# Edge convolution on one core: x picked in two exact float32r parts by two matmuls a tile, node keys in SBUF, narrow sums, 20 picked steps, a ring of six

## What is computed

```python
xn  = (x - mean) * rsqrt(var + 1e-5) * gamma + beta
feat = concatenate([xn[dst], xn[src] - xn[dst]], axis=-1)       # (200000, 128)
msg = relu(feat @ W1 + b1) @ W2 + b2                            # (200000, 64)
agg = segment_max(msg, dst, num_segments=6250); agg = where(isfinite(agg), agg, 0)
out = layernorm(x + relu(agg))                                  # over the 64 channels
```

## Time and profile before

| | |
|---|---|
| median of 3 runs | 1803.86 us (1803.62 to 1804.23) |
| the profiled execution | 1801.84 us, its span 1800.1 us |
| PE | 1721.3 us busy (96%) |
| POOL | 1317.6 us (73%) |
| DVE | 1197.9 us (67%) |
| ACT | 939.6 us (52%) |
| mean granted clock of TensorE | 0.977 of full speed |

### The profile page before, as it was taken

One profiled execution on the slowest core, in us unless ns is written; L12 is line 12 of the kernel. 1 busy time (PEld: TensorE's weight loads), 2 busy tenths in 40 slices (PEclk: granted clock), 3 DMA queues, 4 the chain that ended last, 5 costly groups with the idle time before them and its releaser, 6 DMA issues.

```text
span 1800.1 us, 26957 instructions
## 1 busy us (share of the span) xinstructions
PE 1721.3 (96%) x9871; PEld 851.8 (47%) x9871; DVE 1197.9 (67%) x1951; ACT 939.6 (52%) x1111; POOL 1317.6 (73%) x1388
## 2 busy tenths in 40 slices
PE   4489999999999999999999999999999999999995
PEld 3244444444444444444444444444445445444442
DVE  5556676666766766667667667676676676666753
ACT  4545555545455545555555555555555555555553
POOL 7777777777777777777777777777777777777722
PEclk8589999999999999999999999999999999999998
DMA  7633343334334333343343333343333433343320
GB/s 180 176 94 93 67 98 88 75 82 96 79 82 97 72 96 79 86 96 67 85 94 96 83 82 93 73 95 70 97 89 65 104 83 85 79 99 81 70 55 5
DMA packets 131566, 156.85 MB, mean 87 GB/s; under 512 B 74988, under 2 KB 76969, under 8 KB 131400
## 3 DMA queue, kind: packets, MB, share of 16 engines
q1 hardware_dynamic: 85674, 109.73, 19.6%
q0 software_dynamic: 44464, 45.18, 17.0%
q10 hardware_dynamic: 1294, 0.20, 0.1%
HBM read 147.24 MB, written 9.39 MB: 87 GB/s over the span
## 4 chain that ended last, share of the span: by engine, by line
PE 94%; DVE 2%; SPq 1%; DMA 1%; ACT 1%; ACTq 1%; issue 0%; POOLq 0%; POOL 0%; DVEq 0%
PE ps_g L1074 29%; PE ps_g L1081 15%; PE ps_acc L1149 11%; PE ps_mr L1118 11%; PE ps_h L1140 10%; PE ps_mr L1124 5%; PE ps_h L1133 5%; PE ps_x L1110 4%; PE ps_h L1138 2%; DMA src_t<-in_src 1%; DMA a_dram<-oh 1%; DVE runmax L939 0%; PE ps_x L1037 0%; SPq L336 0%; SPq L351 0%
## 5 line engine op out<-in xcount | busy, mean ns | idle before, releaser
L473 POOL DMA_INDIRECT xs<-in_x,src_ix x1372 | 1304.8, 951 | 420.4 <-issue 417.3
L865 DVE TENSOR_SCALAR oh<-ps_k 128x1024 bf16<-128x1024 bf16 x1176 | 731.9, 679 | 0.8
L1074 PE MATMUL ps_g<-oh,xtab 128*128 128x512 bf16 x2352 | 541.1, 380 | 0.0
L635 ACT ACTIVATE rows<-ps_mr 128x512 f32<-128x512 f32 x196 | 116.8, 596 | 554.5 <-PE ps_mr L1124 545.1
L939 DVE TENSOR_TENSOR_SCAN runmax<-rb,runmax,ps_mr 128x512 f32<-128x512 bf16 x196 | 250.6, 1278 | 181.2 <-PE ps_mr L1118 180.3
L1074 PEld LDWEIGHTS ps_g<-oh,xtab 128*128 128x128 bf16 x2352 | 217.0, 98 | 301.9 <-issue 68.9
L640 ACT ACTIVATE hid<-ps_h,bias 128x1024 f32<-128x1024 f32 x196 | 218.2, 1113 | 175.0 <-PE ps_h L1140 139.1
L1081 PE MATMUL ps_g<-oh,xtab 128*64 128x512 bf16 x2352 | 289.7, 383 | 0.0
L922 DVE TENSOR_TENSOR best<-ps_acc,last_key 128x336 f32<-128x336 f32 x196 | 99.5, 508 | 282.0 <-PE ps_mr L1124 264.2
L1149 PEld LDWEIGHTS ps_acc<-rows,best 128*106 128x106 f32 x1568 | 183.0, 172 | 160.1 <-issue 155.8
L596 ACT ACTIVATE best<-best,ones 126x1024 bf16<-126x1024 bf16 x196 | 225.1, 1149 | 6.4
(11 more groups left out here) (162 smaller groups left out, 584.6 us busy)
## 6 DMA issues: line engine op xcount, KB each, us to landing
kb<-keys_dram SPq DMA_DIRECT2D x98, 504.0 KB
rb<-reset_dram SPq DMA_DIRECT2D x98, 256.0 KB
xs<-in_x,src_ix POOLq DMA_INDIRECT x1372
src_t<-in_src SPq DMA_DIRECT2D x48, 256.0 KB, 6.7
aw<-a_dram SPq DMA_DIRECT2D x196, 31.5 KB
a_dram<-oh SPq DMA_DIRECT2D x6, 672.0 KB, 3.9
xwin<-xp_dram SPq DMA_DIRECT2D x196, 10.5 KB
out<-y SPq DMA_DIRECT2D x182, 10.5 KB
```

Of the source, the lines that this page charges most:

```text
L473: pool.indirect_dma_start(xs[:, u, t, h, :], None, x[:, :], bass.IndirectOffsetOnAxis(ap=src_ix[:, b, q + t, h:h + 1], axis=0))\
L865: dve.tensor_scalar(oh[0:PN, n % NOH, :], node_keys_ps, n % TN + 0.5, None, ALU.is_equal).then_inc(oh_ready, 1)
L1074: last = pe.matmul(ps_g[:, h, :], xtab[0:PN, t, 0:2, :].rearrange("p w c -> p (w c)"), oh[0:PN, n % NOH, h * GE:(h + 1) * GE], start=t == ...
```

## The change

- **x in two parts.** xtab holds x as two float32r parts: the upper 12 bits (a bitwise and with -4096) and what is left. One wide matmul for each half picks both; the narrow matmuls are gone. The one-hots are float32r too. DVE makes both parts in the first steps (three small instructions a piece), ACT none.
- **Node keys in SBUF.** Two tiles of keys in `best`, used in turn; the copy into ps_k is gone and `node_onehot` reads SBUF. ACT makes keys m only after the one-hots of segment m-2.
- **Narrow sums.** For each of four groups of edges and each half, a float32 matmul of 128 x 42 with 128 x 65, the halves in columns 0 and 64 of the array. Seven windows fit in one bank, so `add_bias` runs once for seven windows.
- **Sizes.** 20 picked steps instead of 24 (980 tiles instead of 1176, at most 6 a step instead of 8, 176 gathered steps), a ring of 9 one-hots instead of 14 with 3 ahead instead of 6, and a ring of 6 steps of gathered rows instead of 12.

```diff
+    UPPER = -(2 ** 12)
-    NOH = 14
-    AHEAD = 6
-    PICKED = 24
+    NOH = 9
+    AHEAD = 3
+    PICKED = 20
...
-    NX = 12
+    NX = 6
...
-        fill.append(max(0, min(want, 8, (len(picked) + 1) * TN - tiles, total - tiles)))
+        fill.append(max(0, min(want, 6, (len(picked) + 1) * TN - tiles, total - tiles)))
...
-        xtab = sb("xtab", [P, TN, NPC, C], bf16)
+        xtab = sb("xtab", [P, TN, 2, C], f32r)
+        x_upper = sb("x_upper", [P, 2, TG, C])
...
+        oh = sb("oh", [P, NOH, 2 * GE], f32r)
...
-        node_key = best[0:PN, 0:GE].bitcast(bf16)
+        node_key = [best[0:PN, 0:GE].bitcast(bf16), best[0:PN, 9 * GE:10 * GE].bitcast(bf16)]
...
             def node_keys(m):
                 act.wait_ge(src_b_in, 32 * m + 32)
-                if m > 0:
-                    act.wait_ge(node_ps, m)
-                act.activation(node_key, src_b, ACT.Identity, bias=node0[0:PN, :]).then_inc(node_key_ready, 1)
+                if m > 1:
+                    act.wait_ge(oh_ready, (m - 1) * TN)
+                act.activation(node_key[m % 2], src_b, ACT.Identity, bias=node0[0:PN, :]).then_inc(node_key_ready, 1)
...
-            for g in range(4, XG):
-                x_hi_piece(g)
...
-                    act.activation(xtab[0:PN, t0:t1, 1, :], xn[0:PN, t0:t1, :], ACT.Copy).then_inc(x_mid, 1)
...
+            chain(dve.memset(ps_acc[:, 0:GE - SL], 0.0))
...
-                def take_nodes(m):
-                    dve.wait_ge(node_key_ready, m + 1)
-                    if m > 0:
-                        dve.wait_ge(oh_ready, m * TN)
-                    dve.tensor_copy(ps_k[0:PN, :], node_key.bitcast(f32)).then_inc(node_ps, 1)
-                    dve.wait_ge(node_ps, m + 1)
...
+                    dve.tensor_scalar(x_upper[0:PN, g % 2, 0:t1 - t0, :].bitcast(i32), xn[0:PN, t0:t1, :].bitcast(i32), UPPER, None,
+                                      ALU.bitwise_and).then_inc(x_up, 1)
...
+                def x_parts(g):
                     t0, t1 = g * TG, min(TN, g * TG + TG)
+                    dve.wait_ge(x_up, g + 1)
+                    dve.tensor_copy(xtab[0:PN, t0:t1, 0, :], x_upper[0:PN, g % 2, 0:t1 - t0, :]).then_inc(x_hi, 1)
+                    dve.tensor_tensor(xtab[0:PN, t0:t1, 1, :], xn[0:PN, t0:t1, :], x_upper[0:PN, g % 2, 0:t1 - t0, :],
+                                      ALU.subtract).then_inc(x_lo, 1)
...
                 def node_onehot(n):
                     if n % TN == 0:
-                        take_nodes(n // TN)
-                    dve.tensor_scalar(oh[0:PN, n % NOH, :], node_keys_ps, n % TN + 0.5, None, ALU.is_equal).then_inc(oh_ready, 1)
...
+                        dve.wait_ge(node_key_ready, n // TN + 1)
+                    dve.tensor_scalar(oh[0:PN, n % NOH, :], node_key[n // TN % 2], n % TN + 0.5, None, ALU.is_equal).then_inc(oh_ready, 1)
...
-                def narrow(n):
-                    for h in range(2):
-                        pe.matmul(ps_g[h * C:(h + 1) * C, h, :], xtab[0:PN, n % TN, 2, :],
-                                  oh[0:PN, n % NOH, h * GE:(h + 1) * GE], start=False, stop=False)
...
                     for t in range(TG):
-                        last = pe.matmul(ps_acc[0:ROWS, q * NR:(q + 1) * NR], pick_cols[:, j % 2, t, 0:ROWS], rows[:, j % 2, t, :],
-                                         start=(i == 0 and t == 0), stop=(i == WI - 1 and t == TG - 1))
+                        for h in range(2):
+                            last = pe.matmul(ps_acc[h * 64:h * 64 + SL, p * C1:(p + 1) * C1], pick[:, j % 2, t * 2 + h, :],
+                                             rows[:, j % 2, t * 2 + h, :], start=(i == 0 and t == 0),
+                                             stop=(i == WI - 1 and t == TG - 1))
```

More of the change, by code:

```diff
@@ L7, in edge_conv_program @@
 def edge_conv_program(nc, x, src, dst, gamma, beta, W1, b1, W2, b2, out):
-    f32, i32, bf16 = mybir.dt.float32, mybir.dt.int32, mybir.dt.bfloat16
+    f32, i32, bf16, f32r = mybir.dt.float32, mybir.dt.int32, mybir.dt.bfloat16, mybir.dt.float32r
     ALU, ACT, AX = mybir.AluOpType, mybir.ActivationFunctionType, mybir.AxisListType
@@ L78, in edge_conv_program @@
     gathered = [k for k in range(NI) if k not in picked]
[L79 to L84, removed]
     ends = {w1 * WI + 2: (n, w0 % WB, w0 % WB + w1 - w0) for n, (w0, w1) in enumerate(GROUPS)}
@@ L159, in edge_conv_program @@
         bn = sb("bn", [P, 6])
-        oh = sb("oh", [P, NOH, 2 * GE], bf16)
+        with nc.sbuf_tensor("a_st", [P, AS, TG, 2, NPC, HID], bf16) as a_st:
+            pass
+        oh = sb("oh", [P, NOH, 2 * GE], f32r)
         node0 = sb("node0", [P, 1])
@@ L223, in edge_conv_program @@
         ps_k = pb("ps_k", [P, GE])
+        acc_v = ps_acc[0:ROWS, 0:WB * C1].rearrange("p (w c) -> p w c", c=C1)
         slots_ps = ps_acc[:, GE - SL:GE]
@@ L243, in edge_conv_program @@
         cols_ready = sem("cols_ready")
-        x_hi, x_rest, x_mid, x_lo = sem("x_hi"), sem("x_rest"), sem("x_mid"), sem("x_lo")
+        x_up, x_hi, x_lo = sem("x_up"), sem("x_hi"), sem("x_lo")
         src_first, src_in, dst_in = sem("src_first"), sem("src_in"), sem("dst_in")
@@ L634, in take_rows @@
                     act.wait_ge(turn_ps, j + 1)
-                    act.activation(rows[:, j % 2, :, 0:2 * C], ps_mr[:, :].rearrange("p (t c) -> p t c", t=TG),
+                    act.activation(rows[:, j % 2, :, 0:C], ps_mr[:, :].rearrange("p (t c) -> p t c", c=C),
                                    ACT.Copy).then_inc(rows_sb, 1)
@@ L874, in add_bias @@
-                    dve.wait_ge(added, subs[0] * 3 - 2)
-                    for p0, p1 in ((0, 64), (64, ROWS)):
-                        dve.tensor_tensor(sums[p0:p1, c0:c1, :], acc_v[p0:p1, :, p0:p0 + C], bias2[p0:p1, c0:c1, :], ALU.add).then_inc(added, 1)
+                    dve.wait_ge(added, n * 2 + 1)
+                    dve.tensor_tensor(sums[:, c0:c1, :], acc_v[:, c0:c1, 0:C], bias2[:, c0:c1, :], ALU.add).then_inc(added, 1)
                 def norm_sum(n, c0, c1):
                     wn = c1 - c0
-                    dve.wait_ge(added, subs[0] * 3)
+                    dve.wait_ge(added, n * 2 + 2)
@@ L905, in norm_scale @@
                                       ALU.mult).then_inc(y_ready, 1)
-                chain(dve.memset(best[:, 5 * GE:7 * GE], 0.0))
-                subs = [0]
                 n = 0
@@ L916, in _ @@
                         dve.wait_ge(turn_ps, k - 1)
-                    if k in sub_ends:
-                        add_bias(*sub_ends[k])
+                    if k in ends:
+                        add_bias(*ends[k])
                     if 2 <= k <= NI + 1:
@@ L921, in _ @@
                             dve.wait_ge(last_ready, len(LAST_GROUPS))
-                        dve.tensor_tensor(pick[:, k % 2, :, 0:SL], slots_v,
+                            chain(dve.memset(rows[:, :, :, C:C1], 1.0))
+                        dve.tensor_tensor(pick[:, k % 2, :, :], slots_v,
                                           last_key[:, k - 2, :, :].rearrange("p t h -> p (t h)")
@@ L941, in _ @@
                     for g in range(2 * k, min(2 * k + 2, XG)):
-                        x_rest_piece(g)
-                    for g in range(max(0, 2 * k - 2), min(2 * k, XG)):
-                        x_lo_piece(g)
+                        x_upper_piece(g)
+                    for g in range(2 * k, min(2 * k + 2, XG)):
+                        x_parts(g)
                     if k in ends:
@@ L1077, in wide @@
                         last.then_inc(segment_ps, 1)
-                def narrow(n):
-                    for h in range(2):
-                        pe.matmul(ps_g[h * C:(h + 1) * C, h, :], xtab[0:PN, n % TN, 2, :],
-                                  oh[0:PN, n % NOH, h * GE:(h + 1) * GE], start=False, stop=False)
                 def select(n, upto):
-                    if n < upto and n % TN == 0:
-                        parts = (wide, narrow)
-                    else:
-                        parts = (narrow, wide)
                     for m in range(n, upto):
@@ L1092, in select @@
                         pe.wait_ge(oh_ready, m + 1)
-                        parts[0](m)
-                    for m in range(n, upto):
-                        parts[1](m)
+                        wide(m)
                 def last_piece(m, i, h):
```

40 lines of the change are left out of this document (11 added, 29 removed).

## The result

The kernel after takes 1951.02 us (median of 4 runs, 1950.22 to 1951.74), the kernel before beside it 1803.74 (1803.44 to 1804.23): ratio 1.0816, 95% interval 1.0797 to 1.0835, 8.2% slower. The forecast was 1903, within 1800 to 1995. The profiled execution of after has a span of 1948.3 us.

What follows compares the result with a forecast made beforehand. POOL's gathers were taken to bound the kernel: 1727.8 + 39.9 for more gathers + 3 for the ring = 1770.7, + 95 for one-hot locks = 1866, then 1899 at the end and 1903 us with overheads; range 1800 to 1995.

Steps and rivals of the forecast that it cites:

- POOL's end without locks: POOL's last gather: 1727.8 plus 39.9 for 32 more gathers, plus 3 for the smaller ring, gives 1770.7 us.
- the ring: Gathered rows, 6 steps instead of 12: an early gather waits for PE, 4.1 us lost, taken as 3.
- The lock term: SBUF-to-SBUF one-hots on DVE block POOL's gathers: 0.4 us a step or 75 in 188 steps; 95 us taken.
- POOL gets in between two: With one-hots back to back 0.60 us apart, a held gather on POOL enters after one; 0.25 per group of four.
- The upper bound of 207: Most that one-hots could hold POOL's gathers: 1.1 us a step, two full waits, 207 us.
- the lower end of 1835: Lower bound of the main forecast case for the kernel's time, 1835 to 2015 us, chance 0.74.
- The end behind POOL: From POOL's last gather at 1866 to 1899 us: landing 2, last step 3, clock 2, final 23.85, clock 2 more.
- PE's terms: PE: float32r picking one pass, 0.433 a tile, 424 us; sums 0 change (-110 to +140); new loop 1321 us.
- The clock: PE's idle stretches of 3 to 4 us a step may drop the loop's clock; no term. End: lower level.
- R1: Rival, chance 0.14: one-hots hold no gathers; POOL ends at 1770.7, kernel 1803 to 1807, or 1798 if faster.
- R2: Rival, chance 0.08: float32r on PE isn't one pass; two passes 1860 us, float32 price 2790 us.
- R3: Rival, chance 0.04: one-hots on DVE take 1.15 us and still hold gathers, costing 392 us; kernel 2200 us.

Runs made afterwards that it cites:

- The cut kernel with PSUM keys: Kernel after without PE's part of 47 of 49 tiles per segment and half the sums, node keys copied to PSUM: 1800.56 us, ratio to before 0.9978.
- the cut kernel at 1950.11 us: Kernel after without PE's part of 47 of 49 tiles per segment and half the sums, keys in SBUF: 1950.11 us, ratio to before 1.0803.
- with pauses: Kernel after, each one-hot waiting until the one before is complete: 2276.9 and 2260.5 us, against 2379.1 and 2347.4 for before on those chips.

## Why the prediction was right, and which term was mis-sized

- **The bound moves from PE to POOL's gathers**: right. PE waits 378 us for rows, 2.1 a gathered step (forecast: some 3), and POOL pauses but once in the loop. Its mean gather is 1.058 us, where the sum had 1.01.
- **POOL's end without locks, 1770.7**: right. The cut kernel with PSUM keys ends its gathers at 1767.4, with the 32 gathers more and the ring of six. In after the ring cost one wait of 3.4 us, forecast 3.
- **The lock term, 95 us**: right mechanism, too small; 155.1 measured, and this is the term that was mis-sized. Three things lie in the 155.1. The ordinary waits at the first point, which the sum was about, came to 72.0 us, below the 95. "A gather needs something 0.12 after its start ... and then runs its other 0.82" is true of one of two points; those released at the second, 0.12 ahead of the gather's end, lost 26.1 us that the sum didn't have. "POOL gets in between two" held for most; 35 of the 539 held gathers waited for more than one instruction, and these 35 lost 56.5 us. So the total was nearer than its parts, which is luck in part: 23 us too many stand against 83 that were missing. The upper bound of 207, two full waits a step, held; the lower end of 1835 does not follow from the lock bound of 0, which gives 1808. The trace of before showed the second point in the preparation: the gather of 25.72 ended at 27.39, 0.12 behind L796 (27.27), and I had read only the rows that fit one point.

```profile
25.72 1.67 POOL L473 DMA_INDIRECT xs<-in_x,src_ix  x1 [0.30 <-issue]
...
26.04 1.22 DVE L796 TENSOR_SCALAR hid<-step_t 98x2048 bf16<-98x2048 f32 x1
```

- **POOL's end**: 1767.4 + (155.1 - 5.4) = 1917.1, and the trace has 1920.4; forecast 1866.
- **The end behind POOL**: forecast 33, measured 27.9 (1948.3 - 1920.4). The last rows_across starts at 1927.31, 6.9 behind the last gather's end, as forecast (7); from there 21.0 us to the end, not 25.85. The two gaps, 54.4 late at POOL's end and 5.1 early behind it, leave the 49 us of the span.
- **PE's terms**: one pass, right, at 0.244 instead of 0.217; what the 0.027 are, the weights' load or another thing, no run separates. The sums were taken at no change and are 0.51 us a step shorter, 100 us in 196 steps. Both lie beside POOL and cost or gave nothing, which the cut kernel at 1950.11 us shows.
- **The clock**: the text named a drop in the loop and gave it no term. It came: the mean granted clock was 0.88 from 107 to 1920 us, where it was 1.00 in before's loop (105 to 1776), and it cost nothing that shows. "8 us did" reads too much into the earlier trace rows: in before the clock was at 0.50 in most stretches from 50 us on, long ahead of the 8 us in which PE stood. At the end (1920 to 1948 us) it was 0.71, where the forecast took the lower level.
- **The rivals**: R1 fell with 155 us of held gathers, R2 with 0.244 us a matmul, R3 with one-hots of 0.71. R1's sum for a kernel in which nothing is held, 1799.6 + 3.7, comes close to the cut kernel with PSUM keys, 1800.6.

What the change saved on PE, 258 us of busy time, was worth nothing for the reason given ahead: POOL was 48 us behind PE's end. What it cost is one property of the one-hot, both ends in SBUF.

## What to carry to other kernels

Before PE is unloaded, sum up the engine with the steady pitch, pauses of its own included (here 1404 times 1.248): that is the floor. Ahead of moving a vector instruction's source from PSUM to SBUF because it runs faster there, look whether GpSimd issues DMAs beside it. Here each one-hot was 0.5 us shorter than its PSUM form of the same type, and the kernel 150 us longer. A pause between such instructions took away long waits and left the short ones; what it is worth in time wasn't measured where POOL sets the end. Count all points at which the other engine's instruction can be held, not the first that fits.

## What the runs showed of the hardware that was not expected

- A gather of 0.94 us can be held at two points: 0.12 after its start, and 0.82 after it. The first waits for instructions with two sources too: in before's loop 22 gathers end 0.82 behind one, ten of them behind L890, and none of the 22 is over 1.4 us. At the second point mainly instructions with one source and both ends in SBUF were found to hold, the one-hots and L796. The Trainium skill (SBUF — State Buffer, SBUF: two separate sides) has a GpSimd DMA blocked until the vector instruction ends; the trace agrees at both points, and that there are two, and that a gather can wait out four instructions in a row (3.73 us), only the trace shows.
- The one-hots pay as well: some 200 of 980 took 0.79 to 0.82 us instead of 0.67 to 0.70. All 227 of over 0.785 us have a gather's second point 0.15 to 0.28 us after their start, and none of the 712 of up to 0.70 us has.
- A float32r one-hot of 128x1024 from bf16 keys takes 0.68 us from SBUF (the median; 0.69 with pauses) and 1.21 from PSUM, while the bf16 one of before takes 0.68 from PSUM. So leaving the keys where they were would not have been free: 980 x 0.5 = 490 us of DVE.
- Sixteen matmul records of 128x42 by 128x65 take 0.56 us, eight of 128x106 by 128x129 took 1.07.
- With PE's work cut, the mean granted clock fell from 0.865 to 0.736 (keys in SBUF, PE busy for 59% of the span instead of 75%), and the time did not move.
